# Batches 1 to 7 normalised in one pass, its last step on GpSimd, in an attention and mixture-of-experts kernel

## The reference

```python
xn = (x - mean(x)) / sqrt(var(x) + 1e-5)          # over the 128 features
# attention: 16 heads of 8, causal, softmax over 512 keys
h = xn @ W1 + b1;  q, k, v = split(h)
a = softmax(q @ k.T / sqrt(8), causal) @ v;  att = a @ Wp + bp
# experts: 8 experts of 352 hidden, the best 2 per token, and one shared
probs = softmax(xn @ gate_w.T);  topw, topi = top_k(probs, 2);  topw /= topw.sum()
ffn(x, g, u, d) = (silu(x @ g.T) * (x @ u.T)) @ d.T
out = x + att + ffn(xn, shared...) + sum_of_2(topw * ffn(xn, expert...))
```

## Time and profile before

| | |
|---|---|
| runs | 625.11, 628.49, 633.05 us, median 628.49 |
| profiled execution | span 620.2 us; the page gives it no other time |
| TensorE, VectorE busy | 556.2, 431.6 us of the span |
| ScalarE, GpSimd busy | 312.2, 296.8 us |
| mean granted clock of TensorE | 0.903 of 2.4 GHz |
| chain that ended last | PE 70%, DVE 18%, issue 4%, DMA 3%, ACT 3% |
| attention steps end, experts begin | about 390 us |

### The profile page before, as it was taken

One profiled execution on the slowest core, in us unless ns is written; L12 is line 12 of the kernel. 1 busy time (PEld: TensorE's weight loads), 2 busy tenths in 40 slices (PEclk: granted clock), 3 DMA queues, 4 the chain that ended last, 5 costly groups with the idle time before them and its releaser, 6 DMA issues.

```text
span 620.2 us, 13289 instructions
## 1 busy us (share of the span) xinstructions
PE 556.2 (90%) x4236; PEld 359.0 (58%) x4237; DVE 431.6 (70%) x910; ACT 312.2 (50%) x664; POOL 296.8 (48%) x341
## 2 busy tenths in 40 slices
PE   3497778988897999999999997899999999999995
PEld 1255333543352454444445443699999999987773
DVE  7777776587678677876777877355555555547886
ACT  2014445574475487775777775333333333345552
POOL 2021122133233458786786763076666644455442
PEclk9565787897798799997999996799999999999998
DMA  4713213102101103456131110122212222314664
GB/s 117 235 52 128 79 78 129 54 22 88 52 20 52 53 31 124 132 196 171 44 134 50 33 41 26 34 55 65 66 53 68 59 60 68 115 39 137 169 169 135
DMA packets 51577, 53.26 MB, mean 86 GB/s; under 512 B 5360, under 2 KB 38992, under 8 KB 51280
## 3 DMA queue, kind: packets, MB, share of 16 engines
q1 hardware_dynamic: 47184, 43.75, 22.6%
q0 software_dynamic: 4352, 8.95, 4.6%
HBM read 20.38 MB, written 17.90 MB: 62 GB/s over the span
## 4 chain that ended last, share of the span: by engine, by line
PE 70%; DVE 18%; issue 4%; DMA 3%; ACT 3%; DVEq 1%; SPq 0%; POOL 0%; ACTq 0%; POOLq 0%
PE av_bank L737 14%; PE mx_pair L686 10%; PE av_bank L875 8%; DVE neg_max L1295 6%; PE mx_pair L693 6%; PE st_banks L710 5%; PE st_banks L886 4%; DVE o_sb L1445 3%; PE mx_pair L751 3%; PE mx_pair L861 2%; ACT probs L1054 2%; PE mx_pair L862 2%; DMA out<-o_sb 2%; PE mx_pair L865 2%; PE mx_pair L864 2%
## 5 line engine op out<-in xcount | busy, mean ns | idle before, releaser
L1295 DVE TENSOR_REDUCE neg_max<-mx_pair 128x2 f32<-128x256 f32 (+3 forms) x256 | 202.8, 823 | 82.2 <-PE mx_pair L693 81.6
L1054 ACT ACTIVATE probs<-st_banks 128x512 f32<-128x512 f32 (+1 forms) x384 | 180.8, 524 | 117.7 <-PE st_banks L710 117.2
L686 PE MATMUL mx_pair<-k_st,q_st 31*128 31x256 f32 (+3 forms) x512 | 98.6, 423 | 29.9 <-DVE neg_max L1295 28.6
L686 PEld LDWEIGHTS mx_pair<-k_st,q_st 31*128 31x128 f32 x512 | 47.1, 200 | 127.8 <-DVE neg_max L1295 83.7
L591 POOL DMA_INDIRECT y_tok<-y_sb,y_rows x72 | 70.0, 972 | 78.3 <-ACT y_sb L1128 63.8
L710 PE MATMUL st_banks<-q_st,k_st 32*128 32x128 f32 (+3 forms) x512 | 100.2, 423 | 5.8 <-ACT probs L1054 5.8
L737 PE MATMUL av_bank<-probs,v 128*9 128x512 f32 (+3 forms) x1024 | 100.1, 489 | 0.0
L552 POOL DMA_INDIRECT sorted_x<-xn_rows,slot_idx x64 | 62.7, 979 | 15.0 <-issue 14.6
L509 POOL TENSOR_SCALAR_AFFINE_SELECT probs<-probs 128x1024 f32<-128x1024 f32 x32 | 36.4, 1138 | 62.3 <-ACT probs L1054 62.2
L693 PE MATMUL mx_pair<-mask_qk,ident_bf 128*128 128x128 bf16 (+1 forms) x384 | 66.1, 258 | 0.0
L1121 ACT ACTIVATE sg<-mx_pair 128x352 f32<-128x352 f32 x72 | 33.4, 463 | 63.3 <-PE mx_pair L866 63.3
(11 more groups left out here) (191 smaller groups left out, 919.1 us busy)
## 6 DMA issues: line engine op xcount, KB each, us to landing
sorted_x<-zeros SPq DMA_DIRECT2D x8, 580.5 KB, 3.8
xg<-sorted_x SPq DMA_DIRECT2D x36, 129.0 KB, 2.2
q_st<-q_hi SPq DMA_DIRECT2D x16, 256.0 KB, 2.5
k_st<-k_hi SPq DMA_DIRECT2D x16, 256.0 KB, 2.5
picked<-y_tok SPq DMA_DIRECT2D x16, 256.0 KB, 4.0
egu_lo<-in_e_gu SPq DMA_DIRECT2D x2, 1408.0 KB, 7.8
x_all<-in_x SPq DMA_DIRECT2D x8, 256.0 KB, 4.4
q_st<-q_lo SPq DMA_DIRECT2D x8, 256.0 KB, 2.7
```

Of the source, the lines that this page charges most:

```text
L686: pe.matmul(mx_pair[i % 2][:, k, lo:lo + w], q_st[buf][32 * j:32 * j + 31, g, qb * P:(qb + 1) * P], k_st[buf][32 * j:32 * j + 31, g, 0:w], ...
L1054: act.activation(dst, src, ACT.Exp, scale=SCALE).then_inc(st_free, 1)
L1295: ins = dve.tensor_reduce(neg_max[:, g, h:h + 2, qb], mx_pair[i % 2][:, :, lo:lo + (qb + 1) * P], AX.X, ALU.max, negate=True)
```

## The change

VectorE still does batch 0 alone. For batches 1 to 7 it takes the sums one after the other (1 to 3 before `first_low(0)`, 4 between the two `first_low`, 5 to 7 after), then one chain of 11 small instructions on 28 columns, then raises `rstd_set`. GpSimd waits for that and does the 28 subtract-and-scale instructions, ahead of its first `split`. SyncE issues all of `x` ahead of the strips, the gate weights after them. TensorE transposes only batch 0 ahead of the steps; batch 1 stands in step -2 (its query projection after it), batches 2 to 7 in steps -1 to 4. The router's halves stand in steps 4 and 5 instead of -1 and 4, and everything of the routing behind them one step later, the scatters in steps 15 to 30.

```diff
 def first_misc(s):
+    if s == -2:
+        return [("xT", 1)]
+    if s == -1:
+        return [("k", 1), ("v", 0)]
+    if s == 4:
+        return [("lg", 0)]
...
 def second_misc(s):
-    if s == -1:
-        return [("lg", 0)]
-    if 0 <= s < B - EARLY:
-        return [("xT", s + EARLY)]
-    if s == 4:
-        return [("lg", 1)]
+    if s == -2:
+        return [("q", 1)]
+    if -1 <= s < B - 3:
+        return [("xT", s + 3)]
     if s % 4 == 1 and 5 <= s <= 29:
-        return [("feat", (s - 5) // 4)]
+        return [("feat", (s - 5) // 4)] + ([("lg", 1)] if s == 5 else [])
...
             x_in_rows(1)
+            x_in_rows(2)
             sp.wait_ge(rows_set, 1)
             last_rows_in(0)
-            x_in_rows(2)
-            x_in_rows(3)
-            sp.dma_start(gate[:], gate_w).then_inc(gate_ld, 16)
+            for b in range(3, B):
+                x_in_rows(b)
             strips_in(0, 0)
             strips_in(0, 1)
-            for b in range(EARLY, B):
-                x_in_rows(b)
+            sp.dma_start(gate[:], gate_w).then_inc(gate_ld, 16)
...
+            def normal_rows(b):
+                for n in range(b * NB, (b + 1) * NB):
+                    ins = pool.tensor_scalar(xn_rows[:, n, 0:E], x_all[:, n, :], mv[:, n, 0:1], rstd[:, n:n + 1], ALU.subtract, ALU.mult)
+                ins.then_inc(xn_done, 1)
+
             pool.memset(zeros[:], 0.0).then_inc(zeroed, 1)
             number_rows(0)
+            pool.wait_ge(rstd_set, 1)
+            for b in range(1, B):
+                normal_rows(b)
             split(1, 0)
             split(1, 1)
             for s in range(GROUPS):
-                first = 4 * (s - 14)
+                first = 4 * (s - 15)
...
-            for b in range(1, EARLY):
-                x_transposes(b)
             pe.wait_ge(consts, 3)
...
-                if s % 4 == 2 and s <= 22:
+                if s == -2:
+                    x_transposes(1)
+                elif s % 4 == 2 and s <= 22:
                     project((s + 6) // 4, 0)
...
+                if s == 4:
+                    router(0)
...
-                if s == -1:
-                    router(0)
-                if 0 <= s < B - EARLY:
-                    x_transposes(s + EARLY)
-                if s == 4:
-                    router(1)
+                if s == -2:
+                    project(1, 0)
+                if -1 <= s < B - 3:
+                    x_transposes(s + 3)
                 if s % 4 == 1 and 5 <= s <= 29:
                     features((s - 5) // 4)
-                if s == 10:
+                if s == 5:
+                    router(1)
+                if s == 11:
                     count_tokens()
...
-            normal_rows(0)
-            normal_rows(1)
+            row_sums(0)
+            row_scales(slice(0, NB))
+            first_rows()
+            for b in range(1, 4):
+                row_sums(b)
             dve.wait_ge(w_ld, 32)
             first_low(0)
+            row_sums(4)
             first_low(1)
-            normal_rows(2)
-            normal_rows(3)
+            for b in range(5, B):
+                row_sums(b)
+            row_scales(slice(NB, NT))
+            dve.sem_inc(rstd_set, 1)
...
-                if -1 <= s < B - EARLY - 1:
-                    normal_rows(s + EARLY + 1)
-                if s == 5:
+                if s == 6:
                     route_exponents()
```

More of the change, by code:

```diff
@@ L88, in score_fills @@
 def score_fills():
-    order = [("xT", b) for b in range(EARLY)]
+    order = [("xT", 0)]
     for s in range(-2, GROUPS):
@@ L254, in attention_moe_kernel @@
         consts, fill_done, vec_p, stat1, o_half = (sem(n) for n in ("consts", "fill_done", "vec_p", "stat1", "o_half"))
-        xn_done, vec = sem("xn_done"), sem("vec")
+        xn_done, vec, rstd_set = sem("xn_done"), sem("vec"), sem("rstd_set")
         z_ready, e_ready, hot_ready, base_ready, routed = (
@@ L568, in _ @@
                     scatter(first + 3)
-                if s == 12:
+                if s == 13:
                     sum_rows()
                     choose_rows(0)
-                if s == 13:
+                if s == 14:
                     choose_rows(1)
@@ L628, in router @@
                 pe.wait_ge(gate_ld, 16)
-                pe.wait_ge(st_free, max(i - 2, used_up("xT", (half_of + 1) * EARLY - 1)))
+                pe.wait_ge(st_free, max(i - 2, used_up("xT", (half_of + 1) * B // 2 - 1)))
                 for n in range(NT // 2):
@@ L1067, in _ @@
             first_high(1)
-            for b in range(1, EARLY):
-                x_out_of(b)
             for s in range(-2, GROUPS):
@@ L1077, in _ @@
                     exponents(s, (4, 5))
-                if s % 4 == 2 and s <= 22:
+                if s == -2:
+                    x_out_of(1)
+                elif s % 4 == 2 and s <= 22:
                     whole((s + 6) // 4, 0)
@@ L1086, in _ @@
                     values_out((s + 3) // 4)
+                if s == 4:
+                    logits_out(0)
                 if scored:
                     exponents(s, (10, 11))
-                if s == 5:
+                if s == 6:
                     act.wait_ge(z_ready, 1)
                     act.activation(prob[:], logit[:], ACT.Exp).then_inc(e_ready, 1)
[L1092 to L1097, removed]
+                if s == -2:
+                    whole(1, 0)
+                if -1 <= s < B - 3:
+                    x_out_of(s + 3)
                 if s % 4 == 1 and 5 <= s <= 29:
                     features_out((s - 5) // 4)
-                if s == 10:
+                if s == 5:
+                    logits_out(1)
+                if s == 11:
                     counts_out()
@@ L1205, in _, with row_sums @@
             dve.tensor_copy(last_rows[:], last_row[:].broadcast_to([32, S])).then_inc(rows_set, 1)
-            def normal_rows(b):
-                q = slice(b * NB, (b + 1) * NB)
+            def row_sums(b):
                 dve.wait_ge(x_ld[b], 16)
@@ L1216, in normal_rows, with row_scales @@
                 link(ins)
+            def row_scales(q):
                 link(dve.tensor_scalar(var[:, q], mv[:, q, 1], EPS, None, ALU.add))
@@ L1223, in normal_rows, with first_rows @@
                     link(dve.scalar_tensor_tensor(out=rstd[:, q], in0=newton[:, q], scalar=1.5, in1=rstd[:, q], op0=ALU.add, op1=ALU.mult))
-                for n in range(b * NB, (b + 1) * NB):
+            def first_rows():
+                for n in range(NB):
                     ins = dve.tensor_scalar(xn_rows[:, n, 0:E], x_all[:, n, :], mv[:, n, 0:1], rstd[:, n:n + 1], ALU.subtract, ALU.mult)
@@ L1342, in _ @@
                 maxima(s + 2, 3)
-                if -1 <= s < B - EARLY - 1:
-                    normal_rows(s + EARLY + 1)
-                if s == 5:
+                if s == 6:
                     route_exponents()
-                if s == 6:
+                if s == 7:
                     route_probabilities()
                     route_best(0)
-                if s == 7:
+                if s == 8:
                     route_choice(0)
                     route_best(1)
-                if s == 8:
+                if s == 9:
                     route_choice(1)
                     route_chosen()
-                if s == 9:
+                if s == 10:
                     route_weights()
-                if s == 11:
+                if s == 12:
                     route_blocks()
                     route_rows()
-                if s == 12:
+                if s == 13:
                     route_tiles()
```

2 lines of the change are left out of this document (removed).

## The result

| | before | after |
|---|---|---|
| runs beside the forecast | 628.64 us median (625.11 to 633.05) | 602.11 us median (598.38 to 607.13) |
| five more rounds | 627.32 (621.56 to 630.13, 17 runs) | 600.34 (598.35 to 605.78, 6 runs) |
| ratio | 1 | 0.9612 [0.9564, 0.9659]; 0.9601 [0.9556, 0.9647] in the second series |
| span profiled | 620.2 us, clock 0.903 | 605.1 us, clock 0.909; in the second series 597.5 us, clock 0.942 |

The changed kernel is faster by 3.9%. An execution's time is 2 us above its span (607.13 against 605.1). The two profiles of the changed kernel are of executions of 607.13 and 599.56 us.

What follows compares the result with a forecast made beforehand. VectorE's normalisation of batches was taken to stall TensorE. Terms -3.4-4.0-3.4-4.7-5.5+0.65+4.4 = -16.0 us took the span from 620.2 to 604.2; with 8.3 added for the median, 612.5 us, range 602 to 622.

Steps and rivals of the forecast that it cites:

- Rival A: From the first turn on TensorE runs at 2.4 GHz; intervals -1 to 3 are 8.3 us less, 604; chance 0.20.
- B: TensorE's clock stays at 1.2 GHz until step 4; three intervals of 13 us, +8, 620.5; chance 0.23.
- D: Waits of steps 0 to 2 pass to ScalarE's copies; only 2.4 us remain, 626; chance 0.05.
- Start and SP queue: Ahead of the steps: first maximum at 22.5 us, first turn at 34.5, net -3.4; x loads' lateness taken as 0.
- Steps -1 to 4: Intervals of 11.4, 12.0, 10.5, 10.5 and 10.0 us; changes of -4.0, -3.4, -4.7, -5.5 and none.
- Router: Router calls in steps 4 and 5: +0.65 us and +4.4 us, with 3.65 us for the call in step 5.
- GpSimd: 28 row operations moved to GpSimd at 0.3 us each, 8.4 us under cover; bounds 0.288 and 0.453 us.
- My sign of being wrong upwards: GpSimd rows above 0.7 us, or a clock of 0.5 past step 1, would make the forecast wrong upwards.
- my own limit of 0.69: GpSimd's row operation is free under 0.69 us, by step 0's first mask; each further 0.1 us costs 2.8.
- rival C: Slow GpSimd row operations, ahead of splits and step 0's first mask; at 1.8 us each, 643.5; chance 0.05.
- Routing's step: Routing's VectorE work one step later, projections' cover lost and gained: taken as 0, bounds -2 to +2 us.
- From the profile to the median: Around the whole kernel: 8.3 us added, the median 628.49 less the profiled span 620.2.

Runs made afterwards that it cites:

- rows_narrow: Changed kernel with GpSimd's row operations on 16 of the 128 columns, the others filled with a constant: 603.49 us.
- rows_twice: Changed kernel with each of GpSimd's 28 row operations done twice, the second waiting for the first: 628.28 us, ratio 1.0044.
- before_router_late: Kernel before with only the router's halves moved to steps 4 and 5 and all routing and scatters one step later: 627.25 us, ratio 0.9982.
- routing_late: Kernel before with the router's halves left in place and only the routing and scatters behind them one step later: 650.88 us, ratio 1.0052.
- router0_step1: Changed kernel with the router's first half in step 1 instead of step 4: 602.08 us, ratio 0.9598.
- no_shift: Changed kernel with the router's halves in steps 1 and 4 and all routing and scatters in the steps of the kernel before: 606.83 us, ratio 0.9708.
- rows_in_steps: Changed kernel with the 28 row operations on VectorE, batch 1 ahead of the steps, batches 2 to 7 in steps -2 to 3: 612.8 us.

## Why the prediction was right, and where it was off

The sign, the main mechanism and the place of the gain were right. TensorE waited for VectorE's normalisation, and with it gone from the steps the waits are gone. The number was right by luck: 602.11 us lies 0.1 us inside the range of 602 to 622, which had been widened to reach the rivals, 10 us under the forecast and below its own 608 to 617; the second series, 600.34, lies outside. Rival A's 604 is nearest. Its short intervals came in steps 1 to 3 (9.42 and 9.48 us), not before. B falls with the clock of 1.00 there, and D with the waits that are gone.

| part | forecast | first profile | second profile |
|---|---|---|---|
| first turn | 34.5 | 34.29 | 34.29 |
| intervals -1 to 4 | 11.4, 12.0, 10.5, 10.5, 10.0 | 11.02, 10.83, 9.42, 9.48, 9.47 | together 50.08 |
| router intervals | 13.6, 14.1 | 16.15, 16.56 | 13.53, 16.23 |
| end of step 6 | 116.6 | 117.22 | 114.13 |
| steps 6 to 15, change | 0 | -2.40 | -6.73 |
| steps 15 to 30, change | 0 | +1.59 | +1.43 |
| behind step 30, change | 0 | +1.13 | +1.11 |
| span, change | -16.0 | -15.1 | -22.7 |

That -16.0 and -15.1 agree is luck too: errors of several us cancel between the rows.

*Start and SP queue*: right to 0.2 us; no load was late. What the order of the loads or the transposes' place gives by itself was not run. *Steps -1 to 4*: over-priced by 4.2 us together. I put the clock between the two levels; from the turn of step 1 to that of step 4 it was at 2.4 GHz, rival A's case in that part, while step 0 was not.

*Router*: under-priced by 2 to 5 us. The calls took 5.45 and 4.54 us in the first profile, 3.69 and 5.02 in the second, and the earlier trace rows had one at 4.91 in step -1; I took the full-clock 3.65. That is 2.7 of the 5.0 us, and 1.4 of the 2.1; the rest lies in the other work of these two intervals, whose clock was 0.62 to 0.77. The error hid the one of the steps before it in the sum at step 6.

*GpSimd*: the price of 0.3 us was wrong, outside both bounds: 0.783, and twice VectorE's 0.28 would have been too little as well. The one-input select and the two-input operation without scalar columns were not near enough to bound an operation with two of them. My sign of being wrong upwards (over 0.7 us) was there, and by my own limit of 0.69 the 0.776 us from one start to the next should have cost 2.4. It cost nothing that rows_narrow can show, because step 0's mask was due some 3 us later than I had it. But the limit was tied to the wrong work: the write of the maxima of step 0's turn, which SyncE issues behind batch 1's query strips, comes due first. With 1.1 us of cover left, the limit is about 0.82 us for one operation (an estimate: 0.776 and 1.1/28). So rival C was nearer than its 0.05: in rows_twice, at 1.67 us for two operations in a row, the whole gain was lost. That the changed kernel lies within its cover is luck as well.

*Routing's step*: the term set at 0 with bounds of 2 either way. Eleven profiles of kernels with the shift have 95.0 to 99.8 us for steps 6 to 15, three without it 102.07, 103.36 and 104.60. My argument by projections' cover had it only neutral. That the key's split on GpSimd stands in steps 7 and 11 beside VectorE's heaviest work is a likely reason, and was only argued. What it gives in the time of the whole is not settled: before_router_late and routing_late did not get faster. Behind step 15 the shift moves a low clock: the profiles with it lose 2.7 to 3.0 us in steps 27 to 29 and save 2.7 in steps 20 to 22 (not counting the two slower chips). By spans, it gives 1.8 us behind step 6 in before_router_late and 3.6 in router0_step1 against no_shift.

*From the profile to the median*: I added 8.3 us for what lies between them. Only 2.0 of it lies around the span. The profiled execution of before was one of its fastest, 622 us, and usual ones have spans of 625 to 627 at clock 0.893. From usual to usual the gain is 26 to 27 us, from profile to profile 15 to 23. Where a usual execution of before spends the 5 us stays open. This term, 6.3 us too high, is the largest single part of the 10 us between forecast and measurement.

## What to carry to other kernels

Work inserted on an engine that a tightly buffered TensorE waits for cost about its own length here, but beside GpSimd's work it took 1.8 to 3.8 us where 1.1 was planned. Move it ahead of the loop or to an engine whose next deadline is far. To find that deadline, follow everything that stands behind the work, through other engines' queues too: here a write in SyncE's queue came due before the mask. rows_twice, which only lengthens the moved work, is a cheap way to measure the cover. Merge chains of tiny instructions across tiles: 11 instructions on 28 columns take 2.4 us, and 7 times 11 on 4 columns take 15 (an estimate from the 2.2 us of one chain at the start). A forecast made against one profile should ask first where that execution stands among the runs.

## What the runs showed of the hardware that was not expected

GpSimd's subtract-and-multiply with two scalar columns takes 783 ns on 128x128 (after) and 424 ns on 128x16 (rows_narrow). By these two points that is some 370 ns before the first column and 3.2 ns for each (an estimate). On VectorE the same operation on 128x128 takes 342 ns, and in a row of them 0.26 to 0.28 us from one to the next, against GpSimd's 0.776; GpSimd's select of 128x128 takes 288 ns. Beside a GpSimd fill of 3,584 columns one VectorE instruction on 4 columns took 2.93 us instead of 0.17 (rows_narrow), and beside GpSimd's masks and splits a group of four VectorE row operations took up to 3.75 us instead of 1.11 (rows_in_steps). That GpSimd is the cause is argued from the times in both cases.

Two chips ran the kernel before in 626 and 627 us, two others in 652 and 653; in the one profile of it there, 23.3 of 26 additional us are in the scatter steps. On the two faster chips the clock falls at places that moved with the routing's step. The two intervals between the turns of steps 27 and 29 take 9.8 to 10.0 us each in kernels with the shift, at clock 0.83, and 8.53 without it; the two between the turns of steps 20 and 22 take 8.5 and 9.4 us with it, and 10.19 and 10.51 without. The first line is the changed kernel, the others the kernel before.

```profile
325.79:335.82 10.03, 9.60 (x85) 4.13 (x81) 6.97 (x13) 6.11 (x13) 6.26 (x8) 0.83 0.09 29
...
279.73:289.92 10.19, 9.76 (x81) 4.59 (x81) 6.97 (x13) 6.11 (x13) 7.22 (x10) 0.74 0.82 230
289.92:300.43 10.51, 10.51 (x101) 5.09 (x93) 7.06 (x12) 7.06 (x15) 6.17 (x8) 0.93 0.16 43
```
